# A second normalisation and layer moved into the attention loop, through the bank of queries and keys

## What is computed

```
xn = layernorm(x)
q, k, v = split(xn @ Wqkv.T + bqkv)                      # 16 heads of 64
s = q k^T / 8 + q . rel_k[dist]                          # per head, 256 x 256
s = where(s < 32nd largest of its row, -inf, s)
attn = softmax(s)
a1 = attn v + attn . rel_v[dist];  a2 = attn a1;  a3 = attn a2
y = x + (sum_i sigmoid(alpha_i) a_i) @ Wout.T + bout
yn = layernorm(y)
f = yn @ base_w.T + base_b;  g = bf16(softmax(yn @ router_w.T + router_b))
mid = yn @ lora_A
out = y + f + 2 * sum_e g_e (mid @ lora_B[e])            # 8 experts of rank 8
```

## Time and profile before

| | |
|---|---|
| median of 3 runs | 718.81 us |
| profiled execution | 719.82 us |
| its span, first to last instruction | 718.1 us |
| VectorE busy | 684.0 us, 95% |
| TensorE busy | 658.3 us, 92% |
| ScalarE busy | 620.5 us, 86% |
| GpSimd busy | 533.5 us, 74% |
| mean granted TensorE clock | 0.98 of full speed |

### The profile page before, as it was taken

One profiled execution on the slowest core, in us unless ns is written; L12 is line 12 of the kernel. 1 busy time (PEld: TensorE's weight loads), 2 busy tenths in 40 slices (PEclk: granted clock), 3 DMA queues, 4 the chain that ended last, 5 costly groups with the idle time before them and its releaser, 6 DMA issues.

```text
span 718.1 us, 20880 instructions
## 1 busy us (share of the span) xinstructions
PE 658.3 (92%) x5768; PEld 513.4 (72%) x5768; DVE 684.0 (95%) x2841; ACT 620.5 (86%) x1754; POOL 533.5 (74%) x934
## 2 busy tenths in 40 slices
PE   4378999999999999999999999999999999998795
PEld 3266777777777777777777777777777777776574
DVE  6899999999999999999999999999999999999925
ACT  4588999989999899989999899989999899988833
POOL 1588898778777777877787778777878787877411
PEclk9779999999999999999999999999999999999998
DMA  6735455444544455444545454545454445454202
GB/s 204 189 106 160 128 152 154 144 149 141 151 137 148 138 147 150 136 141 144 150 134 151 133 149 137 154 130 149 137 158 140 138 134 160 129 149 116 63 13 58
DMA packets 148338, 98.72 MB, mean 137 GB/s; under 512 B 10624, under 2 KB 147968, under 8 KB 148096
## 3 DMA queue, kind: packets, MB, share of 16 engines
q1 hardware_dynamic: 147920, 97.32, 46.4%
q10 hardware_dynamic: 304, 0.08, 0.1%
HBM read 45.59 MB, written 51.77 MB: 136 GB/s over the span
## 4 chain that ended last, share of the span: by engine, by line
DVE 79%; issue 9%; PE 6%; POOL 2%; DMA 2%; ACT 1%; SPq 0%; DVEq 0%; ACTq 0%; POOLq 0%
DVE top L666 40%; DVE work L672 35%; DMA band_scratch<-zeros 1%; POOL s_sb L322 1%; DVE rinv L653 1%; PE ps_p L885 1%; PE ps_y L902 1%; PE ps_d L871 1%; PE ps_s L965 1%; ACT a_sb L435 1%; DVE stats L688 0%; PE ps_a L800 0%; DMA band_scratch<-band 0%; DMA skew<-band_scratch 0%; DVE x_sb L681 0%
## 5 line engine op out<-in xcount | busy, mean ns | idle before, releaser
L666 DVE MAX8 top<-work 128x8 f32<-128x256 f32 x768 | 285.0, 414 | 0.0
L672 DVE MATCH_REPLACE8 work<-top,work 128x256 f32<-128x256 f32 x512 | 206.1, 411 | 0.0
L322 POOL TENSOR_TENSOR s_sb<-s_sb,pen 128x512 f32<-128x512 f32 x127 | 162.1, 1276 | 55.0 <-ACT pen L425 54.6
L327 POOL TENSOR_SCALAR a_sb<-a_sb,rinv 128x256 f32<-128x256 f32 x254 | 119.6, 482 | 54.6 <-DVE rinv L653 53.7
L435 ACT ACTIVATE a_sb<-s_sb,nmax 128x256 f32<-128x256 f32 x256 | 128.1, 501 | 34.1 <-POOL s_sb L322 26.2
L425 ACT ACTIVATE pen<-s_sb,limit 128x256 f32<-128x256 f32 x254 | 116.5, 512 | 21.7 <-POOL limit L309 21.7
L297 POOL TENSOR_TENSOR s_sb<-s_sb,skew 128x384 f32<-128x384 f32 x128 | 128.6, 1004 | 3.0 <-DMA skew<-band_scratch 3.0
L885 PE MATMUL ps_p<-aT,rows 128*64 128x256 f32 x1024 | 125.1, 385 | 0.9 <-issue 0.5
L672 DVE MATCH_REPLACE8 work<-top,s_sb 128x256 f32<-128x256 f32 x256 | 103.0, 411 | 0.0
L666 DVE MAX8 top<-s_sb 128x8 f32<-128x256 f32 x256 | 94.5, 411 | 3.5 <-POOL s_sb L297 3.5
L885 PEld LDWEIGHTS ps_p<-aT,rows 128*64 128x64 f32 x1024 | 69.0, 136 | 38.5 <-issue 11.9
(11 more groups left out here) (136 smaller groups left out, 1289.9 us busy)
## 6 DMA issues: line engine op xcount, KB each, us to landing
skew<-band_scratch SPq DMA_DIRECT2D x128, 192.0 KB, 2.8
diag_scratch<-a_sb SPq DMA_DIRECT2D x128, 192.0 KB, 2.2
band_scratch<-band SPq DMA_DIRECT2D x128, 191.0 KB, 3.3
diag<-diag_scratch SPq DMA_DIRECT2D x128, 128.0 KB, 2.2
wqkv<-in_wqkv SPq DMA_DIRECT2D x1, 1152.0 KB, 7.7
x_sb<-in_x SPq DMA_DIRECT2D x4, 256.0 KB, 4.9
wout<-in_wout SPq DMA_DIRECT2D x1, 512.0 KB, 5.7
out<-xn SPq DMA_DIRECT2D x1, 512.0 KB, 3.3
```

Source lines behind the costliest of these rows:

```text
L322: nc.gpsimd.tensor_tensor(s_sb[g % 4][:], s_sb[g % 4][:], pen[g % 2][:], ALU.subtract).then_inc(pen_added, 1)
L327: nc.gpsimd.tensor_scalar(a_sb[g % 3][:, t, :], a_sb[g % 3][:, t, :], rinv[g % 2][:, t:t + 1], 1.0, ALU.mult, ALU.mult).then_inc(normed, 1)
L666: nc.vector.max(m[:, t, 8 * n:8 * n + 8], src).then_inc(top_step, 1)
L672: nc.vector.match_replace(work[t][:, n % 2, :], m[:, t, 8 * n:8 * n + 8], src, LOW).then_inc(top_step, 1)
```

## The change

1. Batches 0 to 5 (`INSIDE = B - 2`) get their second normalisation and layer in the loop. For batch b these run in these slots: the residual addition and moments on VectorE as before, and behind them `second_scale` on GpSimd, in slot 8(b+1)+4; `second_normal` on GpSimd in 8(b+1)+5; transposes, layer and copies on TensorE and ScalarE in 8(b+2)+4 (`layer_slot`); the addition of the layer's base to y on GpSimd (`add_base`) in 8(b+2)+6. Batch 6 is normalised in the loop, and passes its layer early in the tail.
2. The transposes and the layer of these batches are written to `ps_qk`. The transposes wait for queries and keys of that slot to be copied, the values of the slot wait for the layer's copy. The bias of these batches enters as a product with the identity, and ScalarE copies the sum to `ffn`; for batches 6 and 7 VectorE adds the bias as before.
3. No square root: GpSimd raises variance + eps to the power -0.5 and makes the shift -mean * rstd; the normalised rows are y * rstd + shift. The table loads around the roots, and the warming operations, go. VectorE still normalises batch 7.
4. In the last slots, which have no queries and keys left, the values of q-1 stand at the slot's start, and the last values in slot 63.
5. Gates and low-rank work of batches 0 to 5 stand directly behind the last search; the last group of the tail holds batches 6 and 7. TensorE's transposes of z and the experts of batches 0 to 5 stand among the last powers.

```diff
-        ps_x = [ps_s0, ps_s1, ps_s0, ps_s1, ps_y]
-        ps_f = [ps_s0, ps_s1, ps_s0, ps_s1, ps_s0, ps_s1, ps_s0, ps_p0]
+        ps_x = [ps_qk] * (B - 2) + [ps_s0, ps_y]
+        ps_f = [ps_qk] * (B - 2) + [ps_s1, ps_p0]
...
+        def layer_slot(q):
+            f = (q - NP - 4) // NP - 1
+            return f if q % NP == 4 and 0 <= f < INSIDE and q < PAIRS else None
...
@@ GpSimd
+            def second_scale(b):
+                i = slice(T * b, T * (b + 1))
+                pool.wait_ge(row_stats, 2 * TILES + 2 * T * (b + 1))
+                nc.gpsimd.tensor_scalar(rstd[:, i], mv[:, i, 1], EPS, 1.0, ALU.add, ALU.mult).then_inc(var2_done, 1)
+                nc.gpsimd.tensor_scalar(shift[:, i], mv[:, i, 0], -1.0, 1.0, ALU.mult, ALU.mult).then_inc(var2_done, 1)
+                pool.wait_ge(var2_done, 2 * (b + 1))
+                nc.gpsimd.tensor_tensor(rstd[:, i], rstd[:, i], halves[:], ALU.pow).then_inc(rstd2_done, 1)
+
+            def second_normal(b):
+                i = slice(T * b, T * (b + 1))
+                pool.wait_ge(rstd2_done, b + 1)
+                nc.gpsimd.tensor_tensor(shift[:, i], shift[:, i], rstd[:, i], ALU.mult).then_inc(shift_done, 1)
+                pool.wait_ge(shift_done, b + 1)
+                for i in range(T * b, T * (b + 1)):
+                    nc.gpsimd.tensor_scalar(yn[:, i, :], y_sb[:, i, :], rstd[:, i:i + 1], shift[:, i:i + 1], ALU.mult,
+                                            ALU.add).then_inc(yn_done, 1)
+
+            def add_base(b):
+                i = slice(T * b, T * (b + 1))
+                pool.wait_ge(f_saved, b + 1)
+                nc.gpsimd.tensor_tensor(y_sb[:, i, :], y_sb[:, i, :], ffn[:, i, 0:DIM], ALU.add).then_inc(by_done, 1)
...
+                if q >= NP + 5 and q % NP == 5:
+                    second_normal(q // NP - 1)
+                if q >= 2 * NP + 6 and q % NP == 6:
+                    add_base(q // NP - 2)
                 if on(q):
                     add_penalty(2 * q)
...
+                if q >= NP + 4 and q % NP == 4:
+                    second_scale(q // NP - 1)
                 if on(q):
                     normalise(2 * q)
...
+            add_base(B - 2)
+            second_scale(B - 1)
+            add_base(B - 1)
@@ ScalarE
+            def save_layer(b):
+                act.wait_ge(f_ready, b + 1)
+                nc.scalar.copy(ffn[:, T * b:T * (b + 1), :].rearrange("p t c -> p (t c)"),
+                               ps_f[b][:, 0:T * FFN]).then_inc(f_saved, 1)
...
                 if on(q + 3):
                     save_queries(q + 3)
+                else:
+                    save_values(q - 1)
...
                     save_diagonals(q - 2)
+                if layer_slot(q) is not None:
+                    save_ynT(layer_slot(q))
                 if on(q + 1):
                     save_scores(q + 1)
...
                     save_first(q - 2)
+                if layer_slot(q) is not None:
+                    save_layer(layer_slot(q))
                 if on(q):
                     exponent(2 * q)
...
-                if q == PAIRS - 2:
-                    act.wait_ge(y_stats, 1)
-                    root(0, DONE)
...
+            gate_weights(0, 0, T * INSIDE)
...
-            gate_weights(0, 0, DONE)
-            nc.scalar.activation(warm[:, 0:1], warm[:, 0:1], ACT.Sqrt).then_inc(warmed, 1)
...
-            root(DONE, TILES)
-            act.wait_ge(warmed, 1)
-            nc.scalar.activation(warm[:, 0:1], warm[:, 0:1], ACT.Exp).then_inc(warmed, 1)
@@ VectorE, behind the loop
             mask_last(HEADS - 1)
-            dve.wait_ge(std2_done, 1)
-            own(nc.vector.reciprocal(rstd[:, 0:DONE], std[:, 0:DONE]))
-            second_normal(0, 4)
+            gate_logits(0, T * INSIDE)
             divide(HEADS - 1)
             normalise_last(HEADS - 1)
-            second_normal(4, DONE)
-            dve.wait_ge(ffn_in, 64)
-            for b in range(B - 1):
-                add_layer_bias(b)
-            low_rank(0, 0, DONE)
+            low_rank(0, 0, T * INSIDE)
+            add_layer_bias(B - 2)
+            send_rows(0, 0, 4)
+            send_rows(1, 4, INSIDE)
             add_projection(B - 1)
             row_moments(B - 1)
...
+            second_normal(TILES - T, TILES)
             add_layer_bias(B - 1)
-            low_rank(1, DONE, TILES)
-            send_rows(2, B - 1, B)
+            gate_logits(T * INSIDE, TILES)
+            low_rank(1, T * INSIDE, TILES)
+            send_rows(2, INSIDE, B)
@@ TensorE
             def values(p):
...
+                if layer_slot(p + 1) is not None:
+                    pe.wait_ge(f_saved, layer_slot(p + 1) + 1)
...
+            def second_columns(b):
+                pe.wait_ge(yn_done, T * (b + 1))
+                if b < INSIDE:
+                    pe.wait_ge(qk_saved, 2 * past(NP * (b + 2) + 7))
+                else:
+                    pe.wait_ge(y_done, b + 1)
+                for t in range(T):
+                    last = transpose(ps_x[b][:, t * P:(t + 1) * P], yn[:, T * b + t, :], ident[:])
+                last.then_inc(ynT_ready, 1)
+
+            def layer(b):
+                pe.wait_ge(ffn_in, 64)
+                pe.wait_ge(ynT_saved, b + 1)
+                for t in range(T):
+                    i = b * T + t
+                    if b < INSIDE:
+                        mm(ps_f[b][:, t * FFN:(t + 1) * FFN], ident[:], bffn[:], start=True, stop=False)
+                    last = mm(ps_f[b][:, t * FFN:(t + 1) * FFN], ynT[:, i * P:(i + 1) * P], wffn[:], start=(b >= INSIDE),
+                              stop=True)
+                last.then_inc(f_ready, 1)
...
+                else:
+                    values(q - 1)
...
                     scores(q + 1)
+                if layer_slot(q) is not None:
+                    second_columns(layer_slot(q))
                 if on(q - 1):
                     attention_columns(2 * q - 2)
...
                     third_power(q - 4)
+                if layer_slot(q) is not None:
+                    layer(layer_slot(q))
                 if on(q - 2):
                     first_power(q - 2)
                 if on(q - 1):
                     attention_columns(2 * q - 1)
+                if on(q - 1) and on(q + 3):
                     values(q - 1)
+                if q == PAIRS - 1:
+                    values(q)
                 if on(q - 4):
                     project(q - 4)
@@ TensorE, behind the loop (new order)
+            attention_columns(2 * q - 2); diagonal_columns(q - 2); second_power(q - 3); third_power(q - 4)
+            attention_columns(2 * q - 1); first_power(q - 2); second_columns(B - 2); powers_back(q)
+            project(q - 4); layer(B - 2); middle_columns(0, 0, 4); middle_columns(1, 4, INSIDE)
+            diagonal_columns(q - 1); second_power(q - 2); first_power(q - 1); third_power(q - 3)
+            powers_back(q + 1); project(q - 3); second_power(q - 1); third_power(q - 2); powers_back(q + 2)
+            experts(0, 0, 4); third_power(q - 1); experts(1, 4, INSIDE); project(q - 2); project(q - 1)
+            second_columns(B - 1); layer(B - 1); middle_columns(2, INSIDE, B); experts(2, INSIDE, B)
```

More of the change, by code:

```diff
@@ L289, in _ @@
             nc.gpsimd.memset(bffn[:, DIM + E_:FFN], 0.0).then_inc(made, 1)
-            nc.gpsimd.memset(warm[:], 1.0).then_inc(made, 1)
+            nc.gpsimd.memset(halves[:], -0.5).then_inc(made, 1)
             def add_skew(g):
@@ L371, in slot @@
                     scale_wout(q - 1, 2, ORDER)
+                if q >= NP + 4 and q % NP == 4:
+                    second_scale(q // NP - 1)
                 if on(q):
                     normalise(2 * q)
[L375 to L381, removed]
+            pool.wait_ge(made, MADE)
             for q in range(-3, PAIRS - 1):
@@ L527, in slot @@
                     save_aT(2 * q - 1)
+                if on(q - 1) and on(q + 3):
                     save_values(q - 1)
+                if q == PAIRS - 1:
+                    save_values(q)
                 if on(q - 2):
                     save_rows(q)
-            def root(a, e):
-                nc.scalar.activation(std[:, a:e], mv[:, a:e, 1], ACT.Sqrt).then_inc(std2_done, 1)
-            def save_ynT(g, a, e):
-                act.wait_ge(ynT_ready, g + 1)
-                nc.scalar.copy(ynT[:, a * P:e * P], ps_x[g][:, 0:(e - a) * P]).then_inc(ynT_saved, 1)
             def gate_weights(i, a, e):
@@ L951, in slot @@
                     powers_back(q)
-            def second_columns(g, a, e):
-                pe.wait_ge(yn_done, e)
-                reach(pe, ynT_saved, g - 1)
-                for i in range(a, e):
-                    last = transpose(ps_x[g][:, (i - a) * P:(i - a + 1) * P], yn[:, i, :], ident[:])
-                last.then_inc(ynT_ready, 1)
-            def layer(b):
-                pe.wait_ge(ynT_saved, 4 if b < B - 1 else 5)
-                reach(pe, f_saved, b - 1)
-                for t in range(T):
-                    i = b * T + t
```

(14 more changed lines are left out.)

76 lines of the change are left out of this document (26 added, 50 removed).

## The result

The changed kernel takes 724.07 us (median of 4 runs, 723.26 to 724.47) against 718.87 us of the kernel before (4 runs, 718.33 to 719.76): ratio 1.0073, 95% interval 1.0059 to 1.0087. It is slower by 5.2 us. Its profiled execution took 724.47 us, with a span of 722.7, 4.6 us longer than that of before.

What follows compares the result with a forecast made beforehand. The prediction took VectorE's top-32 search to bound the loop, with TensorE nearly full. Loop +7.3, root -1.6 and tail -4.9 us gave +0.8 us, a median of 719.6 us; range for 8 in 10: 714.3 to 724.5.

Steps and rivals of the forecast that it cites:

- its own case: The forecast's main case for the whole kernel: loop losses and tail gains cancel, 717 to 722 us, chance 0.42.
- Term A: Layer slot: added products and copies make the first exponent late for VectorE's reciprocal; 0.16 us a batch, bounds 0 and 0.4.
- Term B: Layer slot: values wait for ffn's copy, delaying rows' copy, ramp and second exponent; 0.80 us a batch, bounds 0.3 and 1.2.
- Term C: Slot after the layer: GpSimd's normalisation ahead of the penalty delays the exponent; 0.2 us, bounds 0 to 0.35.
- The sum of the loop: Stalls of all batches in the loop added up: +7.3 us, bounds 0 and 13.
- The root: Slot 62: without the square root's two table loads VectorE's waits of 0.89 and 0.67 us go; -1.56 us.
- The tail: Behind the last search: less TensorE work, earlier low-rank work and shorter normalisation, less two-batch last step; -4.9 us, bounds -3 and -6.
- Rival 1: Loop: stalls mostly absorbed, about 0.4 us a batch left, 2.5 in all; total 714.8 us, chance 0.28.
- Rival 2: Loop: TensorE becomes the bound, lateness carries from slot to slot, 2.1 us a batch; total 725.2 us, chance 0.17.
- Rival 3: Tail gives less, from a power over 1 us or TensorE standing between the last powers; total 722.6 us, chance 0.13.

Runs made afterwards that it cites:

- e2: Changed kernel with ScalarE copying the layer's result ahead of the first power's result instead of behind it; 720.01 us, ratio 1.0009 to the kernel before.
- e4: Changed kernel with both reorderings, layer's copy ahead of the first power's and powers_back ahead of project in layer slots; 716.53 us, ratio 0.9960.
- e3: Changed kernel with TensorE doing powers_back ahead of project in layer slots; 722.79 us, ratio 1.0041 to the kernel before.
- e6: Changed kernel with GpSimd's normalisation spread over two slots, one tile each, and the base addition one slot later; 722.40 us, ratio 1.0053.
- e5: Kernel before with slot 62's square root of 14 tiles replaced by GpSimd's power in slot 63; 717.31 us, ratio 0.9983.
- e1: Changed kernel without the loop's transposes, layers and copies of batches 0 to 5, their ffn a constant; 717.41 us, ratio 0.9976 to the kernel before.

## Why the prediction was right, and where not

The time lies inside the range (714.3 to 724.5), but only 0.4 us from its end. The forecast value was 4.5 us too low, and the band of its own case, 717 to 722, missed; the range holds the time because it had been drawn wide enough to take in the rivals. The mechanism was the forecast one, at the forecast places. Between the forecast +0.8 and the 4.6 us of the spans lie 1.5 us in the loop, 1.7 in the tail and 0.8 in the first slots, where nothing was changed, less 0.2 at the root.

In its working a stall is the distance by which a reciprocal starts behind its due time, so the numbers to set beside it are the shifts and not the listed waits.

**Term A**, the first exponent behind the layer: right in cause, low in size. 0.16 us of shift was forecast, 0.24 is there (0.15 of listed wait); e2 and e4 take it away by its cause.

**Term B**, values behind the copy, rows behind values, ramp behind rows: right in cause, low in size. 0.80 was forecast, 0.94 is there (0.86 of listed wait). TensorE's stop was forecast at 0.68 and is 0.54. Two links have an experiment each: without the first (e2) 0.40 is left, without the second (e3) 0.30, without both (e4) nothing.

**Term C**, GpSimd's normalisation: 0.20 forecast, 0.26 there (0.17 to 0.18 of listed wait), and only a part of the cause: the late exponent alone brings 0.18 (e6). I had costed a tile at 0.375 us by an operation with one scalar from memory; with two it takes 0.44. For batch 5 the forecast was 0.35 and 0.14 is there. That its sum of 1.31 is the forecast 1.3 is luck: A and B are low, and C is high by as much.

**The sum of the loop** was 7.3 and is 8.8. No step of the mechanism failed; each term was sized too small, A by 0.08, B by 0.14 and C by 0.06 us, five times. With the 3.95 us between the two kernels taken off, slot 36 shows where. The first power's result was copied 0.12 us later than worked out (401.23 against 397.16 + 3.95), the first exponent began 0.07 later (402.02 against 398.00 + 3.95), the values 0.15, the rows' copy 0.22 and the second exponent 0.23. So small amounts were lost link by link, on both engines, and none of them is one big error.

A reader of listed waits would be off in the same direction. Each of the three waits is 0.08 to 0.09 us shorter than the shift that it goes with: 0.15, 0.86 and 0.18 of idle time are 0.24, 0.94 and 0.26 of delay. On VectorE one instruction begins before the end of the one ahead (in the loop a reciprocal at 398.97 and the next instruction at 399.04, with 0.15 us of work), and an instruction that had to wait loses that.

**The root** was -1.56 and is -1.80, in the first profile of before; against the second it would be about -1.0. That the second wait hung on the clock, I had not seen.

**The tail** was -4.9 and is -3.2, inside its bounds of -3 and -6; against the second profile of before it is -2.0, outside them. The last search ended 7.9 us later than before (5 to 6 were forecast), and 38.0 us followed it, not 36.5. From the last diagonals to the end of the last projection TensorE needed 13.98 us, not 13.4 (708.17 + 0.61 less 694.80). It is listed busy for all of them, without a wait. The experts of six batches took 1.7 us of them and not 1.5, and the other groups 0.3 more than in the kernel before, in pieces of at most 0.15. The power took 0.70 us and not the 0.2 I had taken: 3.2 us from addition to transposes instead of 2.5. From 2 to 14 elements it grows by 0.16 us an element (0.70 and 2.67 us, e5). The estimate that I had worked out from the Trainium skill ("GPSIMD Engine Reference", section 3.1, about 12 cycles an element where a loop branches on its data), 0.02 us for two elements above the fixed 0.19, does not agree with the trace, where they took 0.51 us more than that. The section does not speak of the power itself. Behind the transposes the two batches cost 1.9 us more instead of 1.4. Of these 0.5 us, 0.22 are the last layer, whose four records took 0.98 instead of 0.76; TensorE had idled 3.24 us before the transposes, against 1.49 before, and the granted clock was then lower. The other 0.3 are spread over the steps that follow. The granted clock in these stretches:

```profile
709.00:713.00 4.00, 0.44 (x2) 0.21 (x3) 1.55 (x7) 0.37 (x1) 1.09 (x3) 1.00 0.10 26
713.00:717.00 4.00, 1.21 (x5) 0.88 (x6) 2.22 (x7) 0.23 (x1) 0.72 (x1) 0.54 0.00 0
```

**Rival 1** (stalls absorbed) did not come. **Rival 2** gave the right total, 725.2, by the wrong way: TensorE's lateness is made up in the second slot after, as forecast (the scores are 1.85 us later than VectorE's shift in slot 37 and 0.03 in slot 38), and e4 has VectorE running at its pace with TensorE 98% busy. **Rival 3** came true in its result, a tail that gives less, but in neither cause: the power took 0.70 us, not over 1, and no wait of TensorE between the last powers is listed. My chance of 0.42 for slower was the largest of the three, but the forecast value stood in the middle one.

## What to carry to other kernels

When work is put into a loop of in-order engines that are nearly full, ask of each inserted instruction what is queued behind it, not how long it takes: here the layers cost 7 us in one order and 0.1 in another (e4 against e1). Copy out first what another engine waits for, and have results that feed a copy in front of long work that feeds nothing. Where an engine is the bound, count each listed wait on it with the overlap that it loses (here 0.08 to 0.09 us each). And where a stretch is to be credited to a change, profile the kernel before twice: here its own tail and first slots moved by 1.3 and 2.2 us.

## What the runs showed of the hardware

The power on GpSimd took 0.70 us for 2 elements a partition (8 times, 703 to 711 ns) and 2.67 us for 14 (once, e5): about 0.16 us an element above some 0.4 us. Other operations with 2 elements took 0.19 us. A scaling of 128x128 took 0.375 us with one operand from memory as scalar (24 times), and 0.44 with two and an addition (14 times).

Two executions of the kernel before had the same idle stretch of 2.96 us on TensorE; behind it the granted clock was 0.61 over 4 us in one, and 1.00 in the other.
